# Expert stages of a macaron block: a table of tags, row numbers fetched by Pool, the wait for an add's landing moved to the scaling

## The reference

```python
x = x + 0.5 * _L0_ffn_ref(_layernorm(x), gate, w0, w1, wo)
x = x + _L0_attn_ref(_layernorm(x), wq_a, q_a_norm_w, wq_b, wkv_a, kv_a_norm_w, wkv_b, attn_wo)
x = x + 0.5 * _L0_ffn_ref(_layernorm(x), gate, w0, w1, wo)
# _L0_ffn_ref, for 8 experts, top 2, hidden width 512:
gate_logits = einsum('bsd,de->bse', x, gate_kernel)
top_k_weights, top_k_indices = top_k(gate_logits, 2); top_k_weights = softmax(top_k_weights)
combine = einsum('bsk,bske->bse', top_k_weights, one_hot(top_k_indices, 8))
h0 = einsum('bsd,edm->bsem', x, w0); h1 = einsum('bsd,edm->bsem', x, w1)
out = einsum('bse,bsem,emd->bsd', combine, silu(h0) * h1, wo)
```

## Time and profile before

| | us |
|---|---|
| median of three runs | 1118.25 |
| the profiled execution | 1107.64 |
| its span, first to last instruction | 1105.4 |
| busy: TensorE matmul | 1035.2 (94%) |
| busy: VectorE | 715.4 (65%) |
| busy: ScalarE | 523.2 (47%) |
| busy: Pool | 476.1 (43%) |
| adding DMAs, issue to landing, median | 3.8 |

### The profile page before, as it was taken

One profiled execution on the slowest core, in us unless ns is written; L12 is line 12 of the kernel. 1 busy time (PEld: TensorE's weight loads), 2 busy tenths in 40 slices (PEclk: granted clock), 3 DMA queues, 4 the chain that ended last, 5 costly groups with the idle time before them and its releaser, 6 DMA issues.

```text
span 1105.4 us, 22942 instructions
## 1 busy us (share of the span) xinstructions
PE 1035.2 (94%) x6292; PEld 815.0 (74%) x6293; DVE 715.4 (65%) x1646; ACT 523.2 (47%) x1139; POOL 476.1 (43%) x418
## 2 busy tenths in 40 slices
PE   4669999999889999999999999999999899999994
PEld 4557888888557777777778777777689568788883
DVE  5364665654477788877887787778456836555552
ACT  1342433432156777767767676776411224333321
POOL 2552344343343654646463644443125603344422
PEclk9999999999999999999999999999999999999998
DMA  9843554432101011110011110011567435544330
GB/s 230 285 144 86 136 123 106 107 56 35 58 0 35 34 40 40 39 40 31 30 39 40 39 40 32 30 37 40 190 206 247 165 116 134 130 108 106 50 56 7
DMA packets 71594, 95.83 MB, mean 87 GB/s; under 512 B 9600, under 2 KB 48640, under 8 KB 71296
## 3 DMA queue, kind: packets, MB, share of 16 engines
q1 hardware_dynamic: 57216, 78.04, 22.7%
q0 software_dynamic: 14304, 16.87, 8.7%
HBM read 64.37 MB, written 34.43 MB: 89 GB/s over the span
## 4 chain that ended last, share of the span: by engine, by line
PE 71%; DMA 14%; issue 6%; POOL 4%; DVE 3%; ACT 1%; POOLq 1%; SPq 0%; DVEq 0%; ACTq 0%
DMA out<-shared,small 13%; PE bank L1708 11%; PE bank L1681 11%; PE bank L1669 5%; PE bank L1670 5%; PE bank L1671 5%; PE bank L1780 5%; PE bank L1492 4%; PE bank L1494 4%; PE bank L1496 4%; POOL rows_by_expert L540 3%; PE bank L1460 2%; PE bank L1656 2%; PE bank L1657 2%; PE bank L1504 2%
## 5 line engine op out<-in xcount | busy, mean ns | idle before, releaser
L869 ACT ACTIVATE shared<-bank,small 128x512 f32<-128x512 f32 x256 | 176.4, 689 | 90.9 <-DVE small L1307 89.9
L1307 DVE TENSOR_REDUCE small<-bank 128x1 f32<-128x512 f32 x256 | 174.5, 684 | 43.1 <-PE bank L1671 42.8
L805 ACT CAST split_rows_and_inner<-bank 128x512 fp32r<-128x512 f32 x78 | 45.7, 586 | 240.3 <-PE bank L1477 240.3
L1681 PE MATMUL bank<-constants,shared 128*128 128x128 f32 x1024 | 155.7, 275 | 2.2 <-ACT shared L869 0.7
L1681 PEld LDWEIGHTS bank<-constants,shared 128*128 128x128 f32 x1024 | 121.9, 140 | 45.0 <-issue 13.6
L1494 PE MATMUL bank<-expert_weights_low,split_rows_and_inner 128*128 x312 | 143.8, 461 | 0.0
L1496 PE MATMUL bank<-expert_weights_high,split_rows_and_inner 128*128 x312 | 142.8, 458 | 0.0
L1492 PE MATMUL bank<-expert_weights_high,split_rows_and_inner 128*128 x312 | 125.2, 401 | 2.8 <-DVE split_rows_and_inner L1110 2.5
L1115 DVE TENSOR_TENSOR split_rows_and_inner<-bank,split_rows_and_inner 128x512 fp32r<-128x512 f32 x78 | 53.9, 691 | 111.7 <-ACT split_rows_and_inner L805 111.6
L1669 PE MATMUL bank<-expert_weights_high,shared_split 128*128 128x512 f32 x256 | 122.9, 480 | 1.6 <-POOL shared_split L612 1.6
L603 POOL TENSOR_TENSOR shared<-shared 128x512 f32<-128x512 f32 x32 | 41.1, 1285 | 189.1 <-DVE shared L1317 182.7
(11 more groups left out here) (191 smaller groups left out, 2201.7 us busy)
## 6 DMA issues: line engine op xcount, KB each, us to landing
expert_weights<-L_ffn_w_kernel SPq DMA_DIRECT2D x32, 512.0 KB, 5.2
shared<-rows_by_expert SPq DMA_DIRECT2D x78, 129.0 KB, 2.1
expert_weights<-L_ffn_wo_kernel SPq DMA_DIRECT2D x16, 512.0 KB, 6.5
shared<-inverse_sums SPq DMA_DIRECT2D x64, 128.0 KB, 2.9
attended_transposed<-shared SPq DMA_DIRECT2D x32, 256.0 KB, 3.0
expert_weights<-attended_transposed SPq DMA_DIRECT2D x2, 2048.0 KB, 10.6
shared<-attended_transposed SPq DMA_DIRECT2D x2, 2048.0 KB, 10.3
rows_by_expert<-empty_rows SPq DMA_DIRECT2D x23, 129.0 KB, 2.0
```

Source lines behind the costliest of these rows:

```text
L869: nc.scalar.activation(prob[k % 4], bank[k % 4][:, :], ACT.Exp, bias=negmax[:, k % 8:k % 8 + 1], accum_out=psum[par][:, hh * GT + qt:hh * ...
L1307: V.tensor_reduce(negmax[:, k % 8:k % 8 + 1], bank[k % 4][:, :], AX.X, ALU.max, negate=True).then_inc(max_ready, 1)
L1681: last = tr(bank[4 + k % 2][:, c * P:(c + 1) * P], prob[k % 4][:, c * P:(c + 1) * P], ident)
```

## The change

The tags of all 39 tiles get places of their own in one table, so that no tag is overwritten. VectorE's tag copy waits for no add; the scaling waits for the landing of the add that used the same `ysb` before. Pool fetches a tile's 128 row numbers from the table into a small buffer `row_of` with a copy of its own, which stands ahead of the waits of the add and behind what Pool issued for the tile before, and waits for that copy. Pool's three waits at the end of the second stage are gone; SyncE's stay.

```diff
-        tag = [tiny([2]) for _ in range(3)]
+        tag = tiny([TILES, 2])
+        row_of = [tiny([1], I32) for _ in range(3)]
...
                         if not last:
                             e = pool.value_load(split_tab[0:1, bass.ds(i * 3 + v + 1, 1)], min_val=0, max_val=E - 1)
+                        pool.wait_ge(tag_sb[f], i * 3 + v + 1)
+                        nc.gpsimd.tensor_copy(row_of[v], tag[:, bass.ds(i * 3 + v, 1), 1:2].rearrange("p a b -> p (a b)").bitcast(I32))\
+                            .then_inc(row_known[f], 1)
                         pool.wait_ge(y_sb[f], i * 3 + v + 1)
+                        pool.wait_ge(row_known[f], i * 6 + v * 2 + 1)
                         prev = (v - 1) % 3
                         pool.wait_ge(added[f][prev], (i + (v > 0)) * 16)
-                        pool.sem_inc(add_due[f], 1)
+                        pool.sem_inc(row_known[f], 1)
                         nc.gpsimd.indirect_dma_start(
                             out=dst, out_offset=bass.IndirectOffsetOnAxis(
-                                ap=tag[v][:, 1:2].bitcast(U32), axis=0),
+                                ap=row_of[v].bitcast(U32), axis=0),
                             in_=ysb[v], in_offset=None, bounds_check=T - 1, oob_is_err=False,
                             compute_op=ALU.add).then_inc(added[f][v], 16)
                         if not last:
...
             add_results(1, out.rearrange("b s d -> (b s) d"))
-            for v in range(3):
-                pool.wait_ge(added[1][v], 16 * TILES // 3)
...
-                def keep_tag(t, i, k):
-
-                    dve.wait_ge(added[f][k % 3], (i + k // 3) * 16)
-                    V.tensor_copy(tag[k % 3].bitcast(I32), xslot[k % 3][:, D:ROW].bitcast(I32)).then_inc(tag_sb[f], 1)
-
-                def scale(t, v):
+                def keep_tag(t, k):
+
+                    V.tensor_copy(tag[:, bass.ds(t, 1), :].rearrange("p a b -> p (a b)").bitcast(I32),
+                                  xslot[k % 3][:, D:ROW].bitcast(I32)).then_inc(tag_sb[f], 1)
+
+                def scale(t, i, v):
 
                     dve.wait_ge(y_psum[f], t + 1)
                     dve.wait_ge(tag_sb[f], t + 1)
-                    V.tensor_scalar(ysb[v], bank[7][:, 0:D], tag[v][:, 0:1], None, ALU.mult).then_inc(y_sb[f], 1)
+                    if not isinstance(i, int) or i > 0:
+                        dve.wait_ge(added[f][v], i * 16)
+                    V.tensor_scalar(ysb[v], bank[7][:, 0:D], tag[:, bass.ds(t, 1), 0:1].rearrange("p a b -> p (a b)"),
+                                    None, ALU.mult).then_inc(y_sb[f], 1)
```

More of the change, by code:

```diff
@@ L163, in build @@
         zrow = sb("empty_rows", [P, ROW])
-        small = sb("small", [P, 1088])
+        small = sb("small", [P, 1160])
         shared_at = -(-nc.sbuf_base // 32) * 32
@@ L174, in tiny @@
             used[0] += n
-            assert used[0] <= 1088
+            assert used[0] <= 1160
             if dt != F32:
@@ L319, in build @@
         tag_sb = sems("tag_sb", 2)
-        add_due = sems("add_due", 2)
+        row_known = sems("row_known", 2)
         added = [sems(f"added{f}_", 3) for f in range(2)]
@@ L1150, in step @@
                     multiply(t)
-                    keep_tag(t, i, k)
+                    keep_tag(t, k)
                     if not is_first(i, k):
@@ L1154, in step @@
                             split_low(f, e, 0)
-                        scale(t - 1, (k - 1) % 3)
+                        scale(t - 1, i, (k - 1) % 3)
                         with dve.If(e > 0):
@@ L1165, in moe @@
                 it_low(TILES - 1)
-                scale(TILES - 1, (TILES - 1) % 3)
+                scale(TILES - 1, TILES // 3 - 1, (TILES - 1) % 3)
             own.step(V.memset(carry, 0.0))
```

## The result

In six timed runs of each, before has a median of 1118.72 us (1117.82 to 1121.4) and the changed kernel one of 1128.99 us (1126.07 to 1131.97): ratio 1.0092, 95% interval 1.0071 to 1.0114. It is 10.3 us slower. The forecast was slower by 6.5 us (1124.8, own range 1121.5 to 1128, wide range 1115 to 1131); the measured time lies beyond the own range by 1 us and inside the wide one. The profiled execution took 1127.07 us.

A forecast was written before the change was run, and what follows sets the result against it. The chain of adding DMAs was taken to bound the second expert stage. Moved wait 0, first stage +3.8, second +4.1, DRAIN -1.4 make +6.5 us on 1118.25: 1124.8 us, own range 1121.5 to 1128, wide range 1115 to 1131.

The forecast's parts named there:

- What bounds the stage: Second expert stage: the chain of adding DMAs sets its end, not TensorE; 13% of the span, about 140 us.
- The 2.3 us stall: Second expert stage: two multiplications 7.19 us apart instead of 4.88; the stall goes, but moves nothing at the end.
- The new distance at the outer-lows: Adds around Pool's twelve outer-weight low-part subtractions: 5.08 us apart (4.95 to 5.40), 30.48 per stage.
- dear copy: Rival, chance 0.18: Pool's row copy costs more than forecast, or is held up by VectorE; 1128.5 us.
- upper end of x: Longest time from the end of Pool's outer-weight low-part subtraction to the next add: 1.42 us; 1.10 was taken.
- Stage 1, +3.8 us: First expert stage: its chain of adds grows by 4.3 us; less 0.5 slack, 3.8 pass on to attention.
- Stage 2, +4.1 us: Second expert stage: its chain of adds grows by 4.1 us (3.4 to 6.0), with no slack at the end.
- the adds meet the expert loads better: Rival, chance 0.12: in both expert stages eight loads each cost the adds 1 us less; 1113.8 us.
- DRAIN, -1.4 us: Pool's closing DRAIN without the last waits: 1.4 us if length stays, 2.9 if clocked from issue, 0 if awaiting DMA.
- The moved wait, 0 us: VectorE's wait goes from tag to scaling: TensorE is freed, but the adds set the end, so 0 us.
- The new wait closes: VectorE's scaling wait: open at nearly every tile, closing only beyond 10.6 us; each closing costs TensorE up to 1 us.
- The table and its addresses, 0 us: A few more register steps in VectorE's queue, hidden behind its wait for ScalarE: 0 us.

The follow-up runs named there:

- the change again: The changed kernel, unchanged, timed and profiled a second time against the kernel before: 1131.70 us, ratio 1.0114.
- fourth group: Later runs beside the kernel before at 1118.95 us: the copy alone, the changed kernel with 15 and with 20 filler matmuls, and the moved wait alone.
- the copy alone: Changed kernel with the old wait back at the tag, none at the scaling, Pool's last three waits kept: 1114.14 us (1.0049), later 1126.55 us (1.0058).
- second group: Earlier runs beside the kernel before at 1108.60 us, on another chip; they varied Pool's row copy, its place and who makes it.
- the third profile: Profile of the changed kernel, unchanged, from its third timing, against the kernel before at 1118.95 us: 1129.84 us, ratio 1.0102.
- two copies: Changed kernel with Pool's row copy issued twice in a row, the add waiting for both: 1131.79 us, ratio 1.0114 to the kernel before.
- the moved wait alone: Changed kernel with row numbers copied by VectorE, no copy on Pool, and Pool's last three waits kept: 1117.58 us, 0.9999 to the kernel before.
- The kernel with the last waits back: Changed kernel with Pool's three last waits kept: 1132.35 us, ratio 1.0116 to the kernel before.
- the copy ahead of the outer-low: Changed kernel with Pool's row copy for the next tile issued before its outer-weight low-part subtraction: 1109.52 us, 1.0007 to the kernel before.

## Why the prediction was right in its sign and short in its size

- *What bounds the stage.* Right: the moved wait without a copy on Pool is 0.9999, and delaying the adds alone costs 5.5 and 7.6 us. The 2.3 us stall shows less than I read from it. It is gone in the first profile of the change, but two profiles with the old wait have none either, and the change again has a pair 6.14 us apart.
- *The new distance at the outer-lows*, forecast 5.08 us and 30.48 per stage: 30.20 and 30.92 measured, 5.03 us each in the first. The number came out for a partly wrong reason. I had the copy begin behind the outer-low and take 0.15 us, below the 0.40 of its upper bound. Its record is 0.75 us, beyond both bounds, but it overlaps the outer-low's, and what it adds is 0.16 us behind that end and then the 0.86 (131.94 to 132.80) until the next add starts. The rival "dear copy" took a copy of up to 0.40 us at its full price, or one held by VectorE; doubling the copy refutes the price: 0.11 us more. Its 1128.5 us lie near the measured 1129.0 by luck. (Its upper end of x leaves out the 0.03 us of the third item: 1.45, not 1.42.)
- *Stage 1, +3.8 us*: measured +6.0. The distances brought 4.2 (30.2 on average against 26.0, three profiles each), less the 0.5 of slack. The step that was mis-sized is that all other adds keep their flights: summed over the stage the flights (issue to landing) grew by 1.9 us (156.6 on average against 154.7). 4.2 - 0.5 + 1.9 = 5.6 of the 6.0. The three profiles of either set span 155.9 to 157.8 and 153.6 to 156.2, so a part of the 1.9 can be spread.
- *Stage 2, +4.1 us*: measured +3.2. Distances +4.0 (30.9 against 26.9), flights -1.3, 2.7 in all. The rival "the adds meet the expert loads better" needed 8 us; what the flights show is 1.9 more in one stage and 1.3 less in the other. That these sums belong to the loads is argued, not shown: the long adds stand beside loads in both kernels (5.6 to 7.5 us before, 5.5 to 7.4 after), the sums are hardly larger than what one kernel's profiles differ by, and no run took the loads away.
- *DRAIN, -1.4 us*: -1.42 in every profile without the waits, and 0.9991 (0.9979 to 1.0003) timed. But none of my three ways is what happens, and that the middle one gave the number is luck. It does not keep its 7.55 us: it starts 0.22 us before the last add's record and lasts 9.36, so it starts 3.2 us earlier and takes 1.8 longer:

```profile
1115.77 1.58 POOL L569 DMA_INDIRECT out<-shared,small  x1 [1.92 <-POOLq L568]
```
```profile
L134 POOLq DRAIN  x1: 9361/9361/9361, 1115.5 to 1115.5; - x1
```

- *The moved wait, 0 us.* This step failed, and it is the largest miss. I asked what the freed stall does to the chain of adds and said nothing comes of it; I did not ask what the old wait does when the adds come later. It holds TensorE back with them. Without it TensorE ends its stage when it did before, the adds land 6 us later, and filler that ended 0.13 us after the normalization now ends 4 to 6 us before it. The sum had the 3.8 us pass on at this join and nothing added behind it; the middle part grew by 3.0 us. The sentence "a gap of 4 us after TensorE's filler may also cost clock" stood under a rival; it belonged into the sum. The fourth group closes with it: the copy alone costs 7.6 us, the gap 4.4, the tail gives 1.4 back, 10.6 us beside 10.9 for the change. Across groups it closes less well: with the 5.5 us of the copy alone in the second group it is 8.5, beside 10.3 and 12.8 in the first and third, and that difference I can't assign.
- *The new wait closes*: I expected it open at nearly every tile, and closed only with adds more than 10.6 us behind their scaling. They were up to 12.9 us behind in the first profile, and it closed:

```profile
DVE shared L1137 <- DMA x_after_moe<-shared,small: 6.8, 5, 2.3
```
```profile
204.80 0.69 DVE L1124 TENSOR_TENSOR shared<-shared,bank 128x512 f32<-128x512 f32 x1
...
210.59 0.69 DVE L1124 TENSOR_TENSOR shared<-shared,bank 128x512 f32<-128x512 f32 x1
...
218.67 0.48 DVE L1137 TENSOR_SCALAR shared<-bank,small 128x256 f32<-128x256 f32 x1 [2.26 <-DMA x_after_moe<-shared,small]
```

  It held VectorE five times in the first stage and once in the second, three and six times in the change again, none and once in the third profile. It spread multiplications to 5.9 us at most (6.1 once in the change again, 7.5 once with two copies), 1.0, 1.3 and 2.7 us beyond the period, where the prediction had up to 1. No effect on the end is seen, and no run isolates one.
- *The table and its addresses, 0 us*: the moved wait alone has them, and a copy more per tile on VectorE, and takes as long as before (0.9999).
- *The rule of the Trainium skill* (SBUF — State Buffer, Who interferes with whom) has more rows for VectorE held by Pool: the tag copy of 967.07, 1.02 us instead of 0.16, and a longer one in the same profile, which ends 0.04 us behind an outer-low (Pool, then VectorE):

```profile
155.25 2.97 POOL L551 TENSOR_TENSOR expert_weights_low<-expert_weights,expert_weights_high  x1
156.26 2.00 DVE L1128 COPY small<-shared 128x2 int32 x1
```

  The other direction, which the prediction had under "dear copy", exists too. In the change's third profile one copy of Pool takes 1.30 us and ends just behind a subtraction of VectorE with two SBUF inputs:

```profile
211.66 1.30 POOL L562 COPY small<-small 128x1 int32 x1
211.71 1.23 DVE L1105 TENSOR_TENSOR expert_weights_low<-expert_weights,expert_weights_high  x1
```

  The rule agrees with this row too. The kernel with the last waits back has one such copy (1.32 us), the copy ahead of the outer-low three (1.09 to 1.81 us), the first profile of the change none (0.88 at most). In the three profiles of the change it costs nothing that is seen: at the twelve outer-lows the distances stay within 4.99 and 5.57 us.

## What to carry to other kernels

In an in-order queue a small instruction that the next one waits for costs by where it stands: here 0.1 us ahead of the long operation, and behind it the 0.86 us of preparation that the long operation used to hide. When a wait is loosened on an engine that does not set the end, follow that engine to the end of its stage: it no longer falls behind together with the slower one, waits longer at the next join, and if it was kept busy there by a counted filler, the filler has to be counted anew. A stall that one profile shows should be looked for in a second one before it is priced: the 2.3 us here were in one of three. Before two profiles are subtracted, cut them at marks that both have; here half the difference of the spans lay ahead of the first changed instruction.

## What the runs showed of the hardware that was not expected

- A Pool copy of 128x1 has a record of 0.74 us on average over all 78, against 0.10 for the 128x1 memset of the earlier trace rows and 0.15 for the same copy on VectorE. Records on Pool overlap: it starts 0.65 us before the instruction ahead of it ends, and a second copy costs 0.11 us. A Pool copy that meets a VectorE subtraction of two SBUF inputs took up to 1.81 us.
- From the sequencer's record on the landing or the copy to the start of the indirect DMA it was 0.79 us (132.01 to 132.80, from the record's end) to 0.85. An add already waiting in the queue started 0.17 us behind the outer-low.
- After 4.2 to 5.7 us in which TensorE did nothing (five profiles), its granted clock was at 0.5 of full speed (1.2 instead of 2.4 GHz) for 7 to 10 us: 308.9 to 315.7 in the changed kernel. After 1.3 us or less the 30 us that follow had 0.88 to 1.00 on average, instead of 0.72 to 0.77. The clock was low also where no gap stood ahead, in attention's first 50 us: 325.9 to 332.8 in the changed kernel, 307.4 to 310.9 in the kernel before.
- The span ends 8.05 us after the last landing where Pool's closing DRAIN starts behind it, and 6.63 where it starts before (6.64 in one).
- The opening of the same program (the copy alone) took 86.5 us in one group of runs and 98.0 in another, on another chip. In the long one of the changed kernel SyncE's instructions stood some 0.7 us apart for a while (69 to 76 us). Why is open.
